# Leaving out the empty slots of a routed layer's gathers and scatters

## The reference, cut to what matters

```python
top_vals, top_idx = jax.lax.top_k(probs, K)              # K = 4 of E = 16 experts
top_vals = top_vals / jnp.maximum(top_vals.sum(-1, keepdims=True), 1e-09)
comb = jnp.zeros((N, E), h.dtype).at[jnp.arange(N)[:, None], top_idx].add(top_vals)
g = jnp.einsum('nh,ehi->eni', h, w_gate)                 # I = 176
u = jnp.einsum('nh,ehi->eni', h, w_up)
y = jnp.einsum('eni,eih->enh', jax.nn.silu(g) * u, w_down)
routed = jnp.einsum('enh,ne->nh', y, comb)
shared = jax.nn.silu(h @ sh_gate) * (h @ sh_up) @ sh_down
return (routed + jax.nn.sigmoid(h @ sh_gate_w) * shared).reshape(orig)
```

## Time and profile before

| what | value |
|---|---|
| median of 3 runs | 419.36 us (419.01, 419.36, 421.94) |
| the profiled execution: its span, the only time that its page gives | 449.4 us |
| PE busy | 409.6 us, 91% |
| DVE busy | 235.8 us, 52% |
| POOL busy | 172.2 us, 38% |
| ACT busy | 151.3 us, 34% |
| POOL's indirect DMAs | 47 gathers, 47 scatters |
| packets of POOL's DMA queue | 4,512 packets, 12.33 MB, 9.2% of the 16 engines |

### The profile page before, as it was taken

One profiled execution on the slowest core, in us unless ns is written; L12 is line 12 of the kernel. 1 busy time (PEld: TensorE's weight loads), 2 busy tenths in 40 slices (PEclk: granted clock), 3 DMA queues, 4 the chain that ended last, 5 costly groups with the idle time before them and its releaser, 6 DMA issues.

```text
span 449.4 us, 6240 instructions
## 1 busy us (share of the span) xinstructions
PE 409.6 (91%) x1978; PEld 340.2 (76%) x1978; DVE 235.8 (52%) x516; ACT 151.3 (34%) x308; POOL 172.2 (38%) x157
## 2 busy tenths in 40 slices
PE   1999999999899999999999995969978898799996
PEld 1877888888688888888787784967867787699875
DVE  6966445545954122211488763744534444466557
ACT  2545333333453443233346261421211212122140
POOL 3510311311225544344321177056656655444400
PEclk9999999999999999999999998899869988899999
DMA  7402443234703233311111686022223223211175
GB/s 227 165 5 59 152 127 119 83 117 141 247 13 118 104 120 117 117 36 35 35 37 55 169 187 186 26 72 84 81 70 95 82 72 78 75 49 61 65 272 214
DMA packets 17208, 46.79 MB, mean 104 GB/s; under 512 B 3466, under 2 KB 6050, under 8 KB 16874
## 3 DMA queue, kind: packets, MB, share of 16 engines
q1 hardware_dynamic: 12666, 34.07, 24.0%
q0 software_dynamic: 4512, 12.33, 9.2%
HBM read 38.10 MB, written 8.29 MB: 103 GB/s over the span
## 4 chain that ended last, share of the span: by engine, by line
PE 82%; DVE 8%; another core or an unknown queue 4%; issue 3%; ACT 2%; DMA 1%; SPq 0%; DVEq 0%; ACTq 0%
PE gu L1192 12%; PE gu L1194 12%; PE gu L1193 11%; PE y L1478 10%; PE y L1192 4%; PE y L1194 4%; PE y L1193 4%; PE gu L1458 4%; PE gu L1462 4%; PE gu L1459 4%; PE gu L1411 2%; PE gu L1470 2%; PE y L1555 2%; PE gu L1391 1%
## 5 line engine op out<-in xcount | busy, mean ns | idle before, releaser
L483 POOL TENSOR_TENSOR w_lo<-w_raw,w_hi 128x512 fp32r<-128x512 f32 (+3 forms) x44 | 52.8, 1220 | 145.9 <-ACT w_hi L552 131.4
L1192 PE MATMUL gu<-act_hi,w_hi 128*128 128x512 f32 x196 | 78.4, 400 | 0.7 <-DVE hid L823 0.7
L1194 PE MATMUL gu<-act_hi,w_lo 128*128 128x512 f32 x196 | 77.0, 393 | 0.0
L1193 PE MATMUL gu<-act_lo,w_hi 128*128 128x512 f32 x196 | 76.8, 392 | 0.0
L526 POOL DMA_INDIRECT y_k<-w_raw,put x47 | 46.2, 983 | 60.2 <-DVE w_raw L1111 51.9
L576 ACT ACTIVATE hid_hi<-hid 128x512 fp32r<-128x512 f32 x46 | 29.0, 632 | 89.5 <-DVE hid L823 48.0
L1458 PE MATMUL gu<-w_hi,xgT 128*128 x94 | 37.3, 398 | 20.9 <-issue 12.1
L1478 PE MATMUL y<-w_dn,t_hidT 88*128 x188 | 54.3, 416 | 1.4 <-DVE t_hidT L1118 1.3
L823 DVE TENSOR_TENSOR hid<-silu,gu 128x512 f32<-128x512 f32 x24 | 16.5, 687 | 65.7 <-PE gu L1194 61.2
L709 ACT ACTIVATE silu<-gu 128x176 f32<-128x176 f32 x47 | 14.9, 317 | 102.7 <-PE gu L1462 76.1
L836 DVE TENSOR_TENSOR hid_lo<-hid,hid_hi 128x512 fp32r<-128x512 f32 x46 | 31.7, 692 | 27.2 <-ACT hid_hi L576 26.3
(11 more groups left out here) (229 smaller groups left out, 714.7 us busy)
## 6 DMA issues: line engine op xcount, KB each, us to landing
w_raw<-in_w_gu SPq DMA_DIRECT2D x16, 352.0 KB, 4.3
w_raw<-in_wc SPq DMA_DIRECT2D x8, 576.0 KB, 3.9
w_raw<-in_w SPq DMA_DIRECT2D x11, 384.0 KB, 3.1
w_raw<-y_k SPq DMA_DIRECT2D x5, 512.0 KB, 6.3
w_raw<-scr SPq DMA_DIRECT2D x8, 256.0 KB, 4.3
w_dn<-in_w_dn SPq DMA_DIRECT2D x1, 1936.0 KB
w_raw<-in_ws SPq DMA_DIRECT2D x5, 384.0 KB, 3.4
w_dn<-y_k SPq DMA_DIRECT2D x3, 512.0 KB, 9.3
```

Of the source, the lines that this page charges most:

```text
L483: nc.gpsimd.tensor_tensor(w_lo[par][:, w], w_raw[par][:, w], w_hi[par][:, w].bitcast(F32), ALU.subtract).then_inc(split, 1)
L1192: T.matmul(out, w[0], x[0], start=start, stop=False)
L1193: T.matmul(out, w[0], x[1], start=False, stop=False)
L1194: return T.matmul(out, w[1], x[0], start=False, stop=stop)
```

## The change

Empty slots now get a row number that lies outside the tensors, and both indirect transfers carry a bound with the instruction to skip what lies above it (`bounds_check`, `oob_is_err=False`). For an empty slot `got` - 1 is -1; masked with 4096 + 1023 that gives 5119, above the gather's bound of 1023, and `put` becomes 4 * 5119 - 1 = 20475, above the scatter's bound of 4095. For a used slot both numbers are what they were. The spare rows and their table go, and with them two small operations of DVE. Since a skipped row leaves what was in the landing place, the two places that nothing had written before are cleared once: the buffer `xg` and the eight upper columns of `r_gate`. POOL does that behind its split of `small`, and its first gather also waits for it. Every bound sits in a register that POOL loads just ahead of the transfer: 94 register moves, one for each indirect DMA, which take over the semaphore wait that the transfer had. All 47 tiles are still computed.

```diff
+EMPTY = N * K1
-CT_DUMP = CT_TOK + NT * K1
-CT_P1 = CT_DUMP + SLOT_TILES
+CT_P1 = CT_TOK + NT * K1
-        empty = sb("empty", [P, SLOT_TILES])
-        y_row = sb("y_row", [P, SLOT_TILES])
...
-        xg = carve(sb("xg", [P, 2 * H]), [H] * 2) + [w[i][:, wide] for w in (w_raw, w_hi, w_lo) for i in range(2)]
+        xg_first = sb("xg", [P, 2 * H])
+        xg = carve(xg_first, [H] * 2) + [w[i][:, wide] for w in (w_raw, w_hi, w_lo) for i in range(2)]
...
+            nc.gpsimd.memset(r_gate[:, :, E0:E1], 0.0).then_inc(t_clear, 1)
+            nc.gpsimd.memset(xg_first[:], 0.0).then_inc(t_clear, 1)
             run_chunks(L0, 2, NC[L0], lambda c, par: low(L0, c, par))
...
-                nc.gpsimd.indirect_dma_start(xg[j], None, d["x2"], bass.IndirectOffsetOnAxis(ap=get[:, i:i + 1], axis=0)
-                                             ).then_inc(t_in[j], 16)
+                nc.gpsimd.indirect_dma_start(xg[j], None, d["x2"], bass.IndirectOffsetOnAxis(ap=get[:, i:i + 1], axis=0),
+                                             bounds_check=N - 1, oob_is_err=False).then_inc(t_in[j], 16)
...
-                nc.gpsimd.indirect_dma_start(d["y_k"], bass.IndirectOffsetOnAxis(ap=put[:, i:i + 1], axis=0), t_out[j], None
-                                             ).then_inc(s_y[j], 16)
+                nc.gpsimd.indirect_dma_start(d["y_k"], bass.IndirectOffsetOnAxis(ap=put[:, i:i + 1], axis=0), t_out[j], None,
+                                             bounds_check=N * K1 - 1, oob_is_err=False).then_inc(s_y[j], 16)
...
             pool.wait_ge(t_get, 1)
+            pool.wait_ge(t_clear, 2)
...
-            chain(V.tensor_scalar(get_i[:], got[:], -1.0, 0.0, ALU.add, ALU.max))
-            V.tensor_scalar(get[:], get_i[:], N - 1, None, ALU.bitwise_and).then_inc(t_get, 1)
+            chain(V.tensor_scalar(get_i[:], got[:], -1.0, None, ALU.add))
+            V.tensor_scalar(get[:], get_i[:], EMPTY | N - 1, None, ALU.bitwise_and).then_inc(t_get, 1)
             shared_low(1, 1)
-            chain(V.scalar_tensor_tensor(out=empty[:], in0=got[:], scalar=0.0, in1=cst1[:, CT_DUMP:CT_DUMP + SLOT_TILES],
-                                         op0=ALU.is_equal, op1=ALU.mult))
             chain(V.tensor_scalar(choice[:], get_i[:], N.bit_length() - 1, None, ALU.arith_shift_right))
-            chain(V.scalar_tensor_tensor(out=y_row[:], in0=get[:], scalar=float(K1), in1=choice[:], op0=ALU.mult, op1=ALU.add))
-            V.tensor_tensor(put[:], y_row[:], empty[:], ALU.add)
+            V.scalar_tensor_tensor(out=put[:], in0=get[:], scalar=float(K1), in1=choice[:], op0=ALU.mult, op1=ALU.add)
...
-    d["y_k"] = nc.dram_tensor("y_k", (N * K1 + RING * P, H), F32, kind="Internal").ap()
+    d["y_k"] = nc.dram_tensor("y_k", (N * K1, H), F32, kind="Internal").ap()
```

More of the change, by code:

```diff
@@ L279, in build @@
         s_bt, s_bc = sem("base_turned"), sem("base_in_sbuf")
-        t_get = sem("get_ready")
+        t_get, t_clear = sem("get_ready"), sem("first_rows_cleared")
         t_in = [sem(f"tile_landed{i}") for i in range(XG)]
@@ L1639 @@
     cst1[:, CT_P1] = np.arange(P) + 1
-    cst1[:, CT_DUMP:CT_DUMP + SLOT_TILES] = N * K1 + np.arange(P)[:, None] + P * (np.arange(SLOT_TILES) % RING)
     sel = np.zeros((CB_N, SPREAD * P), np.float32)
```

## The result

The changed kernel takes 422.25 us in the median of 20 runs (417.72 to 424.86); beside it, the kernel before took 419.62 (20 runs, 417.19 to 421.94). The ratio is 1.0074, with a 95% interval of 1.0045 to 1.0103: slower by 2 to 3 us. Ratios leave out executions that took over 1.5% more than the fastest of their kernel, and they are not the quotients of the medians (here 1.0063). I had forecast 419.0. The time lies inside the range, but what moved it was the slower rival, at about a fifth of the lower of the two prices that I had worked out for it (15 and 24 us).

The account below looks back on a forecast made before the run. The prediction took the kernel as PE-bound from end to end, with POOL the near bound. Its terms summed to 0 on the median of 419.36 us, giving a forecast of 419.0 us, range 412.5 to 433.

Parts of the forecast that it names:

- the slower rival: A bound lengthens POOL's transfers until PE waits on the result buffers: 434 or 443 us; chance 0.26 of over 1% slower.
- item 2: POOL's time for one indirect transfer: taken as 0.97 us unchanged with a bound, so 0 on the total.
- Its own slope: Price of longer POOL transfers while gathers and scatters alternate: every 0.1 us per transfer costs 29 x 0.2 = 5.8 us.
- The lower end of item 2: POOL's transfer time goes by rows moved: 0.66 us on average, pair 1.95 us, winning 2.8 us.
- The slack: How late POOL's scatters may run before PE feels it through the four result buffers: 5.3 us.
- What POOL costs before the change: POOL's 8.1 us of falling behind PE over 29 pairs, less 5.3 us allowed: 2.8 us in an undisturbed run.
- Item 3: The 94 register moves ahead of POOL's transfers: taken as nothing, 17 us at the outer end.
- Items 1, 4, 5: 1: 1,920 slots no longer moved, at most 0.1 us; 4: two POOL MEMSETs, 0; 5: two fewer DVE operations, 0.
- The standstills: PE and ACT waits without a releaser, with slow clock about 36 us of the profiled span; treated as mostly the profiler's.
- faster by relief: Rival: skipping relieves POOL and partly real standstills of up to 6.4 us vanish, 413.0 us; chance 0.20 of over 1% faster.
- The change doesn't do what it says: Rival: in POOL's DMA queue skipped rows still become packets, 4,512 stay, time unchanged at 419.4 us; chance 0.05.
- my mark of 2.7: Sign of the slower rival: POOL's back-to-back scatter and gather pairs above 2.7 us, against 2.56 before.

Follow-up runs that it names:

- the second profile: The kernel before, unchanged, profiled again on a chip where it takes about 420 us: 420.44 us, span 418.6 us.

## Why the prediction was wrong

**The step that failed is item 2**, the one of which it said "This decides". "I take 0.97 unchanged, since these are the same instruction on the same 128 row numbers" was wrong: where gathers and scatters alternate, a transfer in a kernel with bounded gathers takes 1.02 to 1.03 us. The term was put at 0; by the pairs it is 29 x (2.65 - 2.57) = 2.3 us, by the tiles 2.4, by the runs at equal clock 2.6 and 3.2. The mechanism was laid out as the slower rival, "takes a slower path ... POOL runs out of its 5.3 us sooner, and DVE's copy, then PE, waits on the ring of four", and the last two of these, with the pair, are what the traces show; what POOL does longer inside a bounded transfer stays open. Its price was taken from outliers (1.23 and 1.38 us), so it stood at 434 and 443 instead of 422. Its own slope, 5.8 us for each 0.1 us of transfer, would have given 2.3 us for the 0.04 us that a transfer takes more in the mean: right. What I lacked was the small case: the chances had a slower rival over 1% only, though with POOL 0.28 us per tile over PE and 2.8 us already paid, every lengthening counts in full, with no threshold to cross first.

**The lower end of item 2** (time by rows moved, 0.66 us) is wrong: a gather of no row takes 1.02 us. The Trainium skill, page "Perfetto Trace Analysis", section "DMA Instruction — SWDGE (GPSIMD)", says that the window of such an instruction is the generation of descriptors; the trace agrees if a skipped row keeps a descriptor, and the packets speak for it: 4,512 as before, with 4 bytes left for each skipped row. My reading of that rule, fewer rows and so fewer descriptors, was the error.

**The slack** of 5.3 us comes out at 6.1 when it is fitted to the tiles; the sum of the prediction gives 6.1 without the 0.8 us that it took off for the scatter's start (9.1 - 0.4 - 2.6), but that this is the reason was not tested. What POOL costs before the change, 2.8 us by the sum, measures 2.2: nearly right, and now seen, in the six waits of 5.5 us and in the 2.2 us that eight buffers give at equal clock.

**Item 3**, the register moves: right at 0. They take 29 ns each, and without them the ratio is the same.

**Items 1, 4, 5**: no difference seen. Fewer bytes give nothing; the two MEMSETs, at 17.25 and 17.34, take 0.15 and 0.52 us in the idle stretch; from DVE's copy of tile 44, at 391.89 in the changed kernel and 392.01 before, it is 26.5 and 26.6 us to the end, so the tail hasn't changed.

**The standstills.** I took them as "mostly the profiler's own", 36 us of the span. They aren't: where the kernel before takes 420 us the profiled spans of all kernels are 412.1 to 423.2 us, and their runs take 416 to 422 in the median. A profiled execution takes 1.8 us more than its span (420.26 for 418.4), so the span of 449.4 us is an execution of about 451, like those on the two chips of 450 us. The standstills came in all three batches on these two and in none on the other three, and the profile that I had looks like that kind while the times beside it were of the other; its own chip isn't on record, so that is an inference. To take them out of the sum was right; the reason was wrong. The rival that built on them (faster by relief) came true in the one run of the changed kernel on such a chip, by 0.7%, but not by skipping.

**"The change doesn't do what it says"**: 4,512 packets did stay, as this rival had it, but 948 of them hold no row, and a third of the bytes went.

**What would show it**: pairs of 2.65 us lay just under my mark of 2.7; scatters starting later and later after the copies (0.8 to 7.9 us) and the wait of L1110 for POOL's transfers were named and came. The first gather at 260.66, later than 257.8, was not a sign against: the kernel before has it at 261.66 in the second profile.

## What to carry to other kernels

When an engine that only issues transfers is slower per step than the bound engine, its surplus times the number of steps, minus the slack of the buffers between them, is time on the path; price an edit to its instruction from the first 0.05 us on, and look at the ring before the instruction. Here the better edit is eight result buffers in the kernel before: 0.9929, against 1.0074 for skipping a third of the rows, both where the kernel before takes 420 us. And if a profiled span is 7% from the timed runs, ask whether both are of the same chip before calling the difference the profiler's.

## What the runs showed of the hardware

- Where gathers and scatters alternate, an indirect transfer of 128 rows with a bound takes POOL 1.02 to 1.03 us against 0.97 (gather) and 0.99 (scatter), whether rows are skipped or not. The bound on the gather also makes the unbounded scatter behind it 1.01 to 1.03. Gathers ahead of all scatters take 1.00 against 0.95 us, scatters behind all gathers 0.98 against 0.97.
- Skipped rows save their bytes, not their packets: 4,512 packets before and after, 12.33 MB and 8.41 MB, 948 packets of 16 bytes for four skipped rows each.
- The gap of 0.30 us before POOL's next transfer takes up small work: one MEMSET of 0.12 us added 0.01 us to the pair, four (0.21 us) 0.05, ten (0.38 us) 0.22.
- The kernel before takes 413.8 to 422.6 us on three chips and 445.3 to 456.7 on two others, and the order of two kernels can be the opposite there.
